# A two-layer conditioned transformer on one core: a fourth bank for scores, one bank for everything else, and row work on other engines

## What is computed

```python
def layer0(x, condition):
    mod = silu(condition) @ Wada + bada
    sh_a, sc_a, gt_a, sh_m, sc_m, gt_m = jnp.split(mod, 6, axis=1)
    xm = layernorm(x, g1, be1) * (1 + sc_a) + sh_a
    x = x + gt_a * attention(xm)      # 16 heads of 16, causal
    xm = layernorm(x, g2, be2) * (1 + sc_m) + sh_m
    return x + gt_m * (gelu(xm @ W1 + b1) @ W2 + b2)

def layer1(x, cond, key_padding_mask):
    normed = adaln(x, cond, w_adaln1)            # layernorm * (1 + scale) + shift
    q, k, v = normed @ wq.T + bq, normed @ wk.T + bk, normed @ wv.T + bv
    scores = q @ k.T / 4, masked by key_padding_mask
    x = x + softmax(scores) @ v @ wo.T + bo      # 16 heads of 16
    normed = adaln(x, cond, w_adaln2)
    return x + gelu(normed @ w1.T + b1) @ w2.T + b2
```

## Time and profile before

| | us |
|---|---|
| three runs | 1122.96, 1128.54, 1132.0 |
| profiled execution, its own time | 1127.04 |
| its span | 1124.9 |
| PE busy, PEld busy | 1051.1, 905.2 |
| DVE, ACT, POOL busy | 828.6, 592.0, 347.9 |

### The profile page before, as it was taken

The page is one execution under the profiler, slowest core; times in us unless marked ns, Lnnn a source line. Parts: engine busy times, 40 slices in busy tenths (PEclk is TensorE's granted clock), DMA queues, the critical chain, the costliest instruction groups (busy, mean ns, idle before and its releaser), DMA issues.

```text
span 1124.9 us, 23896 instructions
## 1 busy us (share of the span) xinstructions
PE 1051.1 (93%) x8588; PEld 905.2 (80%) x8588; DVE 828.6 (74%) x2443; ACT 592.0 (53%) x1143; POOL 347.9 (31%) x333
## 2 busy tenths in 40 slices
PE   3879999999998899999998899999999888999998
PEld 3768888888886688998887787887888667889997
DVE  5478989999897476556638788898889845666553
ACT  1145666666665545433434677777777654344331
POOL 5112343343434544233411132323323343211111
PEclk9689999999999899999997899999999989999999
DMA  7565776757661020000068549466564400100001
GB/s 219 96 95 94 120 151 118 128 102 133 153 103 25 7 62 11 10 11 15 15 98 121 74 74 170 65 95 81 78 97 64 55 2 1 38 20 20 20 19 38
DMA packets 50828, 81.46 MB, mean 72 GB/s; under 512 B 8916, under 2 KB 23476, under 8 KB 49620
## 3 DMA queue, kind: packets, MB, share of 16 engines
q1 hardware_dynamic: 50232, 79.16, 40.3%
q10 hardware_dynamic: 480, 0.79, 0.6%
HBM read 22.64 MB, written 8.44 MB: 28 GB/s over the span
## 4 chain that ended last, share of the span: by engine, by line
PE 71%; DVE 8%; DMA 8%; SPq 5%; issue 4%; ACT 3%; POOL 1%; ACTq 0%; POOLq 0%; DVEq 0%
PE st_bank L576 14%; PE g_bank L576 12%; PE s_bank L576 8%; PE o_bank L576 8%; PE o_bank L664 7%; DMA k_stack<-qk_split 6%; SPq L433 4%; PE st_bank L643 3%; PE s_bank L626 3%; PE s_bank L630 3%; PE st_bank L649 3%; PE st_bank L645 2%; DVE maxima L1141 1%; PE g_bank L684 1%; PE st_bank L644 1%
## 5 line engine op out<-in xcount | busy, mean ns | idle before, releaser
L846 ACT ACTIVATE probs<-st_bank 128x384 f32<-128x384 f32 (+1 forms) x512 | 271.1, 545 | 194.1 <-PE st_bank L645 102.8
L1135 DVE CUSTOM_DVE_ANT_0 s_bank<-s_bank,tri_wide 128x128 f32<-128x128 f32 (+1 forms) x512 | 169.2, 382 | 25.6 <-PE s_bank L627 24.9
L1141 DVE TENSOR_REDUCE maxima<-s_bank 128x2 f32<-128x512 f32 x256 | 166.7, 675 | 24.7 <-PE s_bank L630 24.4
L933 ACT ACTIVATE probs<-st_bank,cols 128x512 f32<-128x512 f32 x112 | 77.2, 689 | 195.0 <-PE st_bank L576 185.1
L576 PE MATMUL st_bank<-qk_split,q_stack 128*128 128x512 f32 x696 | 166.5, 397 | 1.7 <-ACT probs L846 0.9
L576 PEld LDWEIGHTS st_bank<-qk_split,q_stack 128*128 128x128 f32 x696 | 129.3, 188 | 33.7 <-issue 1.9
L576 PE MATMUL g_bank<-xmT,wa 128*128 128x256 f32 x768 | 123.8, 301 | 4.8 <-POOL xmT L1358 4.8
L664 PE MATMUL o_bank<-probs,v_sb 128*32 128x256 f32 (+1 forms) x2048 | 126.1, 365 | 0.1
L630 PE MATMUL s_bank<-k_stack,q_stack 97*128 97x256 f32 x512 | 114.0, 307 | 12.2 <-DMA k_stack<-qk_split 6.9
L630 PEld LDWEIGHTS s_bank<-k_stack,q_stack 97*128 97x128 f32 x512 | 80.9, 196 | 41.1 <-issue 25.5
L649 PE MATMUL st_bank<-q_stack,k_stack 99*128 99x256 f32 x512 | 106.0, 291 | 6.6 <-ACT probs L846 3.3
(11 more groups left out here) (119 smaller groups left out, 2231.3 us busy)
## 6 DMA issues: line engine op xcount, KB each, us to landing
q_stack<-qk_split SPq DMA_DIRECT2D x192, 128.0 KB, 4.6
k_stack<-qk_split SPq DMA_DIRECT2D x186, 128.0 KB, 6.1
gate_rows<-gate_dram SPq DMA_DIRECT2D x32, 128.0 KB, 3.4
w_dram<-w_in SPq DMA_DIRECT2D x8, 512.0 KB, 7.2
wm_f32r<-w_dram SPq DMA_DIRECT2D x4, 1024.0 KB, 11.0
out<-x_sb SPq DMA_DIRECT2D x8, 512.0 KB, 2.9
x_sb<-x_in SPq DMA_DIRECT2D x4, 512.0 KB, 7.5
q_stack<-q_stack SPq DMA_DIRECT2D x4, 384.0 KB
```

The source lines that it names most:

```text
L846: activation(probs[:, h % 8, 0:n], st_bank[h % 2][:, 0:n], ACT.Exp, scale=SCALE)\
L933: activation(h_of[b.const > 0][:, m % 2], h_bank(b, m)[:, :], ACT.Gelu, bias=cols[:, cb + m:cb + m + 1]).then_inc(m_gelu, 1)
L1135: last = v.tensor_tensor_reduce(out=bank[:, keys], in0=bank[:, keys], in1=tri_wide[:, T - (i + 1) * P:T], scale=1.0, scalar=LOWEST, op0=AL ...
L1141: v.reduce_max(maxima[:, gb.mod(2), :, slot], bank[:].rearrange("p (i n) -> p i n", n=T), AX.X).then_inc(max_done, 1)
```

## The change

- `s_bank` has four banks instead of three, `g_bank` one instead of two. All of q, k, v, xT, proj share it, and `take` waits for the user just before: k for q_lo, v for k_lo, xT for v_copied, proj for xm_high, q for y_copied.
- Slots: q 1, 2; k 4, 6; v 8, 9; xT 11; proj 14, 15; on DVE turn 14 and 7, scale 4 and 8, turn_back 9; on ACT attention's high part 10.
- The maxima are transposed by DVE (one 128x64 instruction in `negative_maximum`, at the end of the step) into blocks of 32, and sent by four transfers of 32 partitions each; PE's and ACT's part of it are gone.
- `row_normalise` of the loop's steps is done by POOL, both tiles by `tensor_scalar`, right after the deviation. The opening and the first rows of layer 1 stay on DVE.
- `turn_back` is one instruction over both halves; POOL's `attention_low` is two instead of one.
- SP loads the gates after k's transfers instead of before q's.
- Opening: rows and projections of batches 0 and 1 are made ahead of the loop (v of batch 1 in step 2), which starts at t = 2; the modulation products are spread over the slots of step 2 (`set_up(s)`) and go to o_bank.

```diff
-S_BANK = [h % 3 for h in range(H - 1)] + [1]
+SCORE_BANKS = 4
+S_BANK = [h % SCORE_BANKS for h in range(H)]
-SLOT = {"q": (0, 1), "negmaxT": 1, "k": (3, 5), "v": (6, 7), "xT": 12, "proj": (12, 14)}
-TURN, SCALED, TURN_BACK, ATTN_HIGH, PROJ_OUT = (14, 6), (0, 7), (2, 8), 9, 15
+SLOT = {"q": (1, 2), "k": (4, 6), "v": (8, 9), "xT": 11, "proj": (14, 15)}
+TURN, SCALED, TURN_BACK, ATTN_HIGH, PROJ_OUT = (14, 7), (4, 8), 9, 10, 15
...
-        g_bank = [bank(f"g_bank{i}") for i in range(2)]
+        g_bank = bank("g_bank")
...
-                    when(negmaxT_copied, g.count(1, 1))
-                    for e in range(2):
-                        sp.dma_start(q_stack[ROW_MAX + e:ROW_MAX + e + 1, stack_of(g)].bitcast(fp32),
-                                     negmaxT[H * e:H * (e + 1)].bitcast(fp32)).then_inc(max_loaded[g.mod(2)], 16)
-                    if layer == 0:
-                        when(x_added, c.count(1, -1))
-                        load_gates(c, 0)
+                    when(negmax_turned, g.count(1, 1))
+                    rows = q_stack[ROW_MAX:ROW_MAX + 2, stack_of(g)].bitcast(fp32)\
+                        .rearrange("e s (i b n) -> e s i b n", i=NT, n=32)
+                    for blk in range(P // 32):
+                        sp.dma_start(rows[:, :, :, blk], negmaxT[32 * blk:32 * (blk + 1)])\
+                            .then_inc(max_loaded[g.mod(2)], 16)
...
+                if layer == 0 and c.within(B):
+                    if c.const == 0:
+                        store_tables()
+                    when(x_added, c.count(1, -1))
+                    load_gates(c, 0)
...
-            USES = [("q", 1, 1, q_lo, 1), ("negmaxT", 0, 3, negmaxT_copied, 1), ("k", 0, 1, k_lo, 1),
-                    ("v", 1, 1, v_copied, 1), ("xT", 1, 0, xm_high, 1), ("proj", 0, 4, y_copied, 1)]
+            USES = [("q", 1, q_lo), ("k", 1, k_lo), ("v", 1, v_copied), ("xT", 0, xm_high), ("proj", 4, y_copied)]
...
+            step(0, Step(0), "new")
+            pe.wait_ge(setup_done, 1)
+            step(0, Step(1), "project")
+            step(0, Step(1), "new")
+            step(0, Step(2), "project")
             for layer in range(LAYERS):
-                for t in steps(B, AHEAD * layer, 5):
+                for t in steps(B, AHEAD, 5):
...
                 v.scalar_tensor_tensor(out=dst[:, :, 1], in0=m, scalar=-1.0, in1=dst[:, :, 0],
                                        op0=ALU.mult, op1=ALU.subtract).then_inc(negmax_ready, 1)
+                dve.wait_ge(negmax_ready, g.count(1, 1))
+                last_batch = g - 1
+                wait(dve, max_loaded[last_batch.mod(2)],
+                     last_batch.half().count(MAX_LOADS * 16, MAX_LOADS * 16) if g.const else None)
+                v.transpose(negmaxT[:].rearrange("p i n -> p (i n)"),
+                            dst.bitcast(fp32).rearrange("p i e s -> p (i e s)")).then_inc(negmax_turned, 1)
...
+            def row_normalise(layer, n):
+                gn = in_layer(layer, n)
+                wait(pool, xT_ready, gn.count(1, -1))
+                pool.wait_ge(rstd_ready, gn.count(1, 1))
+                rows = xrows(n, NT)
+                for i in range(NT):
+                    last = g_.tensor_scalar(xn[:, gn.mod(2), i], rows[:, i * D:(i + 1) * D], mv[:, gn.mod(2), i, 0:1],
+                                            rstd[:, gn.mod(2), i:i + 1], ALU.subtract, ALU.mult)
+                last.then_inc(xn_ready, 1)
```

215 lines of the change are left out of this document (110 added, 105 removed).

## The result

The changed kernel takes 1178.11 us (median of four runs, 1172.8 to 1179.38) beside 1128.35 of before: a ratio of 1.044, 95% interval 1.040 to 1.047. The forecast was 1142, the range 1122 to 1158. The direction was right, the size was not: +50 where +15 was forecast. The profiled execution has a span of 1177.6 (1124.9 before), so 52.7 us have to be found in it.

The account below looks back on a forecast made before the run. Q's and K's queued transfers were taken to set the step, PE and DVE within 1 us. Steps +11.4 and +4.0, maxima -4, opening -1, layer 1's start +4.5 made +14.9 on 1127.0: 1142 us, range 1122 to 1158.

Parts of the forecast that it names:

- The one bank: Steps of both layers: PE waits for q, k and xn's turn to be emptied, 2.0 us (layer 1), 1.0 (layer 0).
- The fourth bank: Scores in the steps: frees PE from DVE by one head; taken as 0, bounds 0 and -8 us.
- POOL's rows: Row normalising in the steps: 1.5 us a step on POOL, upper bound 3.0, under some 6 us of cover; 0.
- rival (c): Steps: DVE is the pace-maker, so 1.4 us less DVE work in 26 steps makes it faster, 1099 us; chance 0.11.
- the -4 of the maxima: scoresT's waits for the maxima: four transfers land about 1 us earlier, so some 4 us come back.
- PE alone then gives 20.7: Layer 1 step: PE's own work of 18.7 us plus 2.0 of waits for the one bank.
- One transfer less ahead of Q in layer 0: Layer 0 steps: gate transfer moved behind K gives -0 to -0.5 us a step, covered by PE.
- With 14.78 us of queue unchanged: Q's and K's twelve transfers still take 14.78 us; transfers alone give steps of 20.8 (layer 1), 19.8 (layer 0).
- 6.4 us late for PE: Start of layer 1: bare waits for emptying, 1.8 us each, less earlier waits; +4.5 after K's wait takes up 1.8.
- Net: Q's transfers start 1.0 us later in layer 1, 0.1 in layer 0: Moved slots: later start of Q's transfers within a step, 1.0 us in layer 1, 0.1 in layer 0.
- Rival (b): Layer 1 steps: K's last transfer lands 7.37 us after its issue whatever Q does; step 21.9, total 1155; chance 0.12.
- The opening's -1: Opening: set-up products spread over step 2 start the first two-batch step earlier on PE; -1 us, bounds -8 and +2.

Follow-up runs that it names:

- The kernel with PE as its bound: The kernel before with the maxima turned by DVE and the third group of probs x V in slot 3 instead of slot 1: 1116.67 us, ratio 0.992.
- the two kernels in which the clock stayed at 1.00 there: Changed kernel, half of DVE's layer 1 low parts left out: 1163.5 us; changed kernel, k of layer 1's first two batches in the fourth score bank: 1168.54.

## Why the prediction was wrong

**Right.** The one bank is waited for between q and k, between k and v, and between xn's turn and proj: from start to start 1.04, 1.04 and 0.4 us in a step of layer 1 for 0.9, 0.9 and 0.2. In the nine steps of layer 0 PE sits idle 0.33 us ahead of v and up to 0.3 ahead of k, for 0.4 each. The fourth bank gives nothing. POOL's rows cost nothing although an instruction takes 1.23 us and not 0.75. Q's transfers start 6.10 us into a layer 1 step; 5.9 was written, but the prediction's own terms, 5.14 and 1.0 more, give 6.1. The transfers alone decide at 20.93 once the banks are put back, for 20.8. DVE is not the pace-maker of rival (c): its busy time in nine steps of layer 0 fell from 162.0 to 148.5 us, and the steps grew.

**Right by luck.** DVE's turn gives 6 us alone, 4 were forecast, but not from shorter waits of scoresT, which grew from 7.3 to 8.9 us. Part of it is Q's start, 0.23 us sooner in a step of layer 1, with the turn of negmax gone from PE's slot 1.

The profiled execution is 38 us longer than the sum had it. By stretch 9 of these are in the eleven steps of layer 1, 5 to 6 in layer 0's steps, 6 at layer 1's start up to batch 19, some 10 at the ends of the two layers' attention, 3 in the opening, and 4 are the -4 of the maxima, which did not come. The steps of the prediction that failed are these.

**PE's own work was too small.** "18.7" and hence "PE alone then gives 20.7". The kernel with PE as its bound shows 19.44 us a step without any wait for a bank, 19.3 of it busy. The sum of pieces, each read once, left out 0.6 to 0.7 us: in that kernel scores and scoresT take 8.3 us of a step from start to start for 7.7, and the eight halves of projections 6.0 for 5.8. With 19.3 in its place and 2.4 of waits the sum is 21.7, and 21.66 was measured. The earlier trace rows had it: PE busy 214.3 in eleven steps, 19.5 a step. PE, and not the transfers, then decides a step of layer 1, 0.86 us above the forecast's 20.8, 9 us in all.

**The gate transfer was not free.** "One transfer less ahead of Q in layer 0: -0 to -0.5 a step, covered by PE", and "With 14.78 us of queue unchanged, transfers alone give ... 19.8 (layer 0)". In layer 0 the transfers decide and PE does not, and from Q's first issue to K's last landing it takes 14.66 us in the mean for 14.05. All nine kernels with the gate's 128 KB behind K's transfers show 14.55 to 14.74, and of the eight with it ahead of Q seven show 14.0 to 14.3 (slots with POOL's rows: 14.6). K's issue at a distance from Q's is not the reason: it stands 3.9 to 5.0 us behind with the gate's place alone and 6.0 behind in the changed kernel with the group moved, and both show 14.66. With Q's start 0.2 later that makes 20.47 for 20.05, some 5 us.

**The clock was left out.** "6.4 us late for PE" at layer 1's start: the waits are of that size, 4 x 1.84 - 2 x 0.42 = 6.5, but 14.0 us were lost from the first q to the first scores (36.7 for 22.7, counted from q's own start, 0.17 ahead of the stretches shown). The other 7.5 are products at half the clock. In the two kernels in which the clock stayed at 1.00 there, the loss is about what their waits make: 5.5 us for 5.0 with 0.39 less in each wait, 2.8 for 2.8 with v's wait gone. How much the clock takes differs from one execution to the next. Two more kernels have the changed kernel's instructions at that place, and its four waits of 1.84: the one with three score banks lost 11.9, the one with the group of probs x V moved 10.3. So the clock's part is 4 to 7.5 us. Nor does the whole time follow the clock's mean: the changed kernel's four runs took 1179.38, 1178.73, 1172.8 and 1177.49 us at 0.951, 0.970, 0.964 and 0.958. At the end of layer 0's attention the clock went from 0.94 to 0.83, in layer 1's from 0.94 to 0.87, with +6.6 and +2.9 us; POOL's rows alone make 2.8 of the first. How much of these two is clock was not separated.

**The price of a slot.** "Net: Q's transfers start 1.0 us later in layer 1, 0.1 in layer 0". Alone in the kernel before, q's slots make it 1.26 and 0.47 (5.51 to 5.98 in the mean of nine steps), which with the starts and ends makes 28 us of span and 31 of the medians, where the prediction's two terms come to 13. The prediction let the bank and the slots share one maximum, and so hid how large the second was: with the bank given back, 35 of 50 us stay. Rival (b), K landing 7.37 us behind its own last issue whatever Q does, is not what happens in layer 1: that time became some 4.7 us in the changed kernel's step (last issue 799.72, landing 804.41).

**Opening and maxima.** The opening's -1 came out at +1.6 by the start of batch 4, POOL's rows with it, and the maxima's transfers are waited for twice as long as before. Why, stays open: DVE's turn alone makes it 8.9 us, and turn, rows on POOL, attention's turn back and opening together 15.2.

What is left over: the parts measured alone (q's slots 26 to 31, one bank 15, gate 0 to 6, DVE's turn -6, rows, fourth bank 0) add up to 35 to 46 of 50. With the whole line of slots, 36, in the place of q's it is 45 to 51. The parts cover each other's waits and need not add up; the opening and attention's turn were not measured alone.

## What to carry to other kernels

Before work is moved by a slot, ask which transfer starts behind it: a step that ends with a queue of transfers gets longer by all that its first issue is late, and moving an unrelated group of matmuls from ahead of that issue to behind it gave 18 us in the changed kernel, and some 4 in the kernel before. Count PE's own work of a step from its busy time over many steps, not from pieces. A transfer put behind the one that is waited for can make that one land later. And look at what the granted clock does behind a bare wait of TensorE, above all at the start of a loop, where several lie close together: here it cost 4 to 7.5 us beside the 6.5 of the waits, and not the same each time.

## What the hardware showed beyond what was expected

The granted clock answers to waits all or nothing, and not by their length alone. Three kernels have the same instructions at layer 1's start: twice two waits of 1.84 us with one projection between them. Five of these six times the clock went from 1.00 to 0.50 (1.2 GHz), once for some 14 us. The sixth time, in the changed kernel with the group of probs x V moved, it stayed at 1.00:

```profile
596.73 1.69 PE L587 MATMUL g_bank<-xmT,wa 128*128 128x256 f32 x12 [1.84 <-DVE qk_split L1097]
600.25 1.69 PE L587 MATMUL g_bank<-wa,xmT 128*128 128x256 f32 x12 [1.84 <-DVE qk_split L1097]
```

Pairs of 1.45, and a wait of 1.84 without the second, left it at 1.00 twice each. But it is not shown that the second wait is what matters: in the changed kernel the clock fell 0.4 us behind the first, before the second began. At the starts of steps four waits of 1.56 to 2.04 us took it down and seven of 1.43 to 2.21 did not. One projection of twelve products cost 1.6 us at the one level and 2.5 to 2.9 at the other.

An emptying in two passes, ACT's and then DVE's, exposes both: ACT is at it for 0.84 us and DVE for 0.87, each with two instructions back to back, and between the two stand 0.03 us. (The 0.35 and 0.36 us of issue in the chain above are no gaps; the first instruction of each pair runs there.) Letting DVE begin on one half while ACT reads the other was not tried: the Trainium skill (PSUM — Partial Sum Buffer, PSUM bank collisions raise a hardware error) rules out two engines at the same 32 partitions of one bank at a time, in different columns too, and no run here shows it.
